# A product-based ranking network on one core: one set of row moves, fields by twos in the first three groups

## The reference, cut to what matters

```python
embed = tables[jnp.arange(26)[None, :], sparse_inputs]        # 2048 x 26 fields x 32, gathered
p   = jnp.einsum('bfe,bge->bfg', embed, embed)                 # inner products of all field pairs
l_z = jnp.einsum('bfe,feh->bh', embed, w_z)                    # 26*32 -> 256
l_p = jnp.einsum('bfg,fgh->bh', p, w_p)                        # 26*26 -> 256
l_1 = relu(concatenate([l_z + l_p + l_b, dense_inputs], -1))   # 256 + 13
h   = relu(l_1 @ W1 + b1)                                      # 128
return sigmoid(h @ Wf + bf)                                    # 2048 x 1
```

## Time and profile before

| | us |
|---|---|
| median of 3 runs | 598.29 |
| span of the profiled execution | 548.8 |
| median less span, what lies around it | 49.5 |
| busy POOL | 409.0 |
| busy DVE | 417.5 |
| busy ACT | 139.7 |
| busy PE (granted clock 0.683 in the mean) | 131.1 |

### The profile page before, as it was taken

One profiled execution on the slowest core, in us unless ns is written; L12 is line 12 of the kernel. 1 busy time (PEld: TensorE's weight loads), 2 busy tenths in 40 slices (PEclk: granted clock), 3 DMA queues, 4 the chain that ended last, 5 costly groups with the idle time before them and its releaser, 6 DMA issues.

```text
span 548.8 us, 1701 instructions
## 1 busy us (share of the span) xinstructions
PE 131.1 (24%) x204; PEld 48.0 (9%) x204; DVE 417.5 (76%) x250; ACT 139.7 (25%) x333; POOL 409.0 (75%) x430
## 2 busy tenths in 40 slices
PE   0000000415334100060465100051433600005067
PEld 0000000201111000020121000020110100002023
DVE  4204199998992369998996419999899547999995
ACT  0000004404551021704452010340455110250323
POOL 6777777777777777777777777777777777777792
PEclk9999999976567555585666655567665555558569
DMA  6222323122122222222112222222112222312220
GB/s 148 21 14 13 13 13 14 13 13 14 14 13 13 13 13 14 13 14 13 13 14 14 13 13 13 13 14 13 14 13 13 14 14 13 14 13 13 13 46 2
DMA packets 19640, 9.56 MB, mean 17 GB/s; under 512 B 9888, under 2 KB 19629, under 8 KB 19629
## 3 DMA queue, kind: packets, MB, share of 16 engines
q0 software_dynamic: 13312, 6.84, 22.4%
q1 hardware_dynamic: 6318, 2.63, 2.1%
HBM read 8.85 MB, written 0.01 MB: 16 GB/s over the span
## 4 chain that ended last, share of the span: by engine, by line
POOL 69%; issue 23%; DVE 6%; DMA 1%; PE 1%; ACT 0%; ACTq 0%; POOLq 0%; DVEq 0%
POOL rows L286 66%; DVE pairs L368 3%; DVE prod L348 2%; POOL prod L302 2%; POOL prod L313 1%; DMA rows<-in_L_rec_tables,which 1%; PE ps_h L643 0%; DMA raw<-in_r_sparse_inputs 0%; DVE pair_rows L404 0%; PE ps_h L680 0%; ACT scores L551 0%; PE ps_copy L692 0%; ACT hidden L537 0%; ACTq L120 0%; DVE pairs_T L395 0%
## 5 line engine op out<-in xcount | busy, mean ns | idle before, releaser
L286 POOL DMA_INDIRECT rows<-in_L_rec_tables,which x416 | 393.5, 946 | 128.4 <-issue 125.8
L348 DVE TENSOR_TENSOR prod<-ps_copy,rows 128x1664 f32<-128x1664 f32 (+12 forms) x103 | 194.2, 1910 | 16.8 <-ACT ps_copy L471 16.8
L368 DVE TENSOR_REDUCE pairs<-prod 128x76 f32<-128x2432 f32 (+13 forms) x73 | 195.3, 2680 | 0.0
L626 PE MATMUL ps_h<-field_rows,wz 128*128 128x512 f32 x96 | 59.4, 784 | 290.3 <-ACT field_rows L482 285.4
L379 DVE STREAM_TRANSPOSE rows_T<-rows 128x512 f32<-128x512 f32 (+1 forms) x28 | 18.6, 663 | 98.1 <-DMA rows<-in_L_rec_tables,which 90.7
L471 ACT COPY ps_copy<-rows 128x128 f32<-128x128 f32 (+2 forms) x63 | 21.2, 336 | 273.3 <-DMA rows<-in_L_rec_tables,which 273.0
L643 PE MATMUL ps_h<-pair_rows,w_pair 96*128 96x512 f32 (+2 forms) x64 | 50.2, 943 | 100.3 <-ACT pair_rows L505 84.4
L482 ACT COPY field_rows<-rows_T 32x512 f32<-32x512 f32 (+1 forms) x112 | 58.7, 524 | 34.9 <-DVE rows_T L379 33.4
L626 PEld LDWEIGHTS ps_h<-field_rows,wz 128*128 128x128 f32 x96 | 23.8, 258 | 328.0 <-issue 292.1
L505 ACT COPY pair_rows<-pairs_T 32x256 f32<-32x256 f32 (+1 forms) x96 | 33.5, 349 | 63.1 <-DVE pairs_T L391 61.9
L643 PEld LDWEIGHTS ps_h<-pair_rows,w_pair 96*128 96x128 f32 (+2 forms) x64 | 17.7, 296 | 130.4 <-ACT pair_rows L505 71.9
(11 more groups left out here) (37 smaller groups left out, 31.7 us busy)
## 6 DMA issues: line engine op xcount, KB each, us to landing
rows<-in_L_rec_tables,which POOLq DMA_INDIRECT x416, 3.4
wz<-in_L_rec_w_z SPq DMA_DIRECT2D x1, 768.0 KB, 5.8
field_rows<-rows_T SPq DMA_DIRECT2D x16, 32.0 KB, 1.9
w_pair<-in_w_low SPq DMA_DIRECT2D x1, 288.0 KB, 5.4
w_back<-in_w_high SPq DMA_DIRECT2D x1, 288.0 KB, 5.7
raw<-in_r_sparse_inputs SPq DMA_DIRECT2D x1, 156.0 KB, 2.2
w<-in_L_rec_W SPq DMA_DIRECT2D x1, 128.0 KB
dense_in<-in_r_dense_inputs SPq DMA_DIRECT2D x1, 104.0 KB, 3.2
```

Source lines behind the costliest of these rows:

```text
L286: nc.gpsimd.indirect_dma_start(rows[:, r % 2, f, k, :], None, table_rows, bass.IndirectOffsetOnAxis(ap=which[:, t, f:f + 1], axis=0),).the ...
L348: ins = nc.vector.tensor_tensor(products(r, s)[:, 0:tiles, at:at + g + 1, :], own.broadcast_to([P, tiles, g + 1, E]), rows[:, r % 2, 0:g + ...
L368: nc.vector.tensor_reduce(pairs[:, 0:tiles, first:end], products(r, s)[:, 0:tiles, :, :], AX.X, ALU.add)\
L626: ins = nc.tensor.matmul(ps_h0[:, h, :], wz[:, j, h * P:(h + 1) * P], field_rows[:, j, :, :, :].rearrange("p q t b -> p (q t b)"), start=( ...
```

## The change

- In groups 0 to 2 fields from 12 on are copied in units of two, and fields from 10 to 23 are multiplied and summed in stages of two; fields 24 and 25 stay single stages. The units per group go from 15 to 10, the stages from 18 to 12. The last group keeps its units and stages.
- In groups 0 to 2 the six row chunks are laid in one set (`MOVES`), by ACT after the group's last field copy, and the three pair blocks in one set (`PAIR_MOVES`) after them. The last group keeps its sets: chunks 0 to 3 by ACT, 4 and 5 by SP, pair blocks 0 and 1, then 2. PE's order follows.
- DVE waits for a free product buffer at every second stage (one stage further ahead), ACT for a free copy bank at every second unit (likewise).
- DVE's `turn_rows` no longer waits for the fields' landing itself, except for the last chunk of the last group, and stands after the multiply of the stage that holds the chunk's last field, in all four groups. `turn_pairs` and the pair sets are counted by group.
- The hidden layers and scores of the previous group are made behind fields 20, 22 and 24 (groups 1, 2) and 12, 13 and 14 (last group), instead of 0, 4 and 8.

```diff
-UNITS = [[(0, 4), (4, 8), (8, 12), (12, 14), (14, 16)] + [(f, f + 1) for f in range(16, 26)]] * (GROUPS - 1) + [FINE]
-STAGES = [[(0, 4), (4, 8), (8, 10), (10, 12), (12, 13), (13, 14)] + [(f, f + 1) for f in range(14, 26)]] * (GROUPS - 1) + [FINE]
+UNITS = [[(0, 4), (4, 8), (8, 12)] + [(f, f + 2) for f in range(12, 26, 2)]] * (GROUPS - 1) + [FINE]
+STAGES = [[(0, 4), (4, 8), (8, 10)] + [(f, f + 2) for f in range(10, 24, 2)] + [(24, 25), (25, 26)]] * (GROUPS - 1) + [FINE]
...
-    MOVES = [(0, 4), (4, MOVED), (MOVED, CH)]
-    NM = len(MOVES)
-    PAIR_MOVES = [(0, 2), (2, 3), (TAIL, TAIL + 1)]
+    LATE_MOVE = (4, MOVED)
+    MOVES = [(0, MOVED)] * (GROUPS - 1) + [(0, LATE_MOVE[0])]
+    NM = 2
+    PAIR_MOVES = [[(0, 3), (TAIL, TAIL + 1)]] * (GROUPS - 1) + [[(0, 2), (2, 3), (TAIL, TAIL + 1)]]
...
@@ multiply
-                if n >= PRODS:
-                    dve.wait_ge(summed, n - PRODS + 1)
+                if n >= PRODS - 1 and n % 2:
+                    dve.wait_ge(summed, n + 1 - PRODS + 1)
...
@@ turn_rows
-                for u in range(unit_of(r, PER * j), unit_of(r, PER * j + n - 1) + 1):
-                    first, end = UNITS[r][u]
-                    dve.wait_ge(landed[r][u], DMA * K * (end - first))
+                if r == ROUNDS - 1 and j == CH - 1:
+                    dve.wait_ge(landed[r][POOL_STAGE], DMA * K)
...
@@ DVE's loop
                     if s < len(STAGES[r]):
-                        for j in range(CH):
-                            if s == stage_of(r, UNITS[r][unit_of(r, PER * j + chunk_fields(j) - 1)][0]):
-                                turn_rows(r, j)
                         if r < ROUNDS - 1 or s != POOL_STAGE:
                             multiply(r, s)
+                        for j in range(CH):
+                            if s == stage_of(r, PER * j + chunk_fields(j) - 1):
+                                turn_rows(r, j)
                     if s:
                         add_up(r, s - 1)
...
@@ copy_fields
-                n = NU * r + u - COPIES
-                if n >= 0:
-                    before = r if u >= COPIES else r - 1
+                n = NU * r + u + 1 - COPIES
+                if n >= 0 and n % 2:
+                    before = r if u + 1 >= COPIES else r - 1
...
@@ ACT's loop, groups 0 to 2
                     if r and first == 0:
                         lay_last_pairs(r - 1)
+                    if r and first == 20:
                         make_hidden0(r - 1)
-                    if r and first == 4:
+                    if r and first == 22:
                         make_hidden1(r - 1)
-                    if r and first == 8:
+                    if r and first == 24:
                         make_scores(r - 1)
-                    if first in (14, 16, 17, 18):
-                        lay_rows(r, 0, (14, 16, 17, 18).index(first))
-                    if 20 <= first < 23:
-                        lay_pairs(r, 0, first - 20)
-                    if first == 23:
-                        lay_rows(r, SP_MOVE, 0)
-                    if first == 24:
-                        lay_rows(r, SP_MOVE, 1)
-                for q in range(2, QUADS):
-                    lay_rows(r, SP_MOVE, q)
+                for q in range(QUADS):
+                    lay_rows(r, q)
                 for u in range(PLACES):
-                    lay_pairs(r, 1, u)
+                    lay_pairs(r, 0, u)
                 lay_last_rows(r)
...
@@ ACT's loop, last group
                     lay_last_pairs(r - 1)
+                if first == 12:
                     make_hidden0(r - 1)
-                if first == 4:
+                if first == 13:
                     make_hidden1(r - 1)
-                if first == 8:
+                if first == 14:
                     make_scores(r - 1)
...
@@ PE's order
-                for j in range(*MOVES[0]):
+                for j in range(LATE_MOVE[0]):
                     sum_lz(r, j)
-                for c in range(*PAIR_MOVES[0]):
-                    sum_lp(r, c)
+                if r == ROUNDS - 1:
+                    for c in range(*PAIR_MOVES[r][0]):
+                        sum_lp(r, c)
                 sum_dense(r)
-                for j in range(*MOVES[1]):
+                for j in range(*LATE_MOVE):
                     sum_lz(r, j)
-                for c in range(*PAIR_MOVES[1]):
+                for c in range(0 if r < ROUNDS - 1 else PAIR_MOVES[r][0][1], TAIL):
                     sum_lp(r, c)

```

More of the change, by code:

```diff
@@ L99, in move_of, with pair_move_of @@
     def move_of(j):
-        return next(m for m, (first, end) in enumerate(MOVES) if first <= j < end)
-    def pair_move_of(c):
-        return next(m for m, (first, end) in enumerate(PAIR_MOVES) if first <= c < end)
+        return j // MOVED
+    def pair_move_of(r, c):
+        return next(m for m, (first, end) in enumerate(PAIR_MOVES[r]) if first <= c < end)
     def block_rows(c):
@@ L206, in pnn_kernel, with last_field @@
         MLP_LOADS = 6
-        PAIR_END = [BLOCK * PAIR_MOVES[0][1], BLOCK * PAIR_MOVES[1][1], NP]
-        FIELD_END = [next(g for g in range(NF) if pairs_before(g + 1) >= end) for end in PAIR_END]
+        def last_field(r, m):
+            first, end = PAIR_MOVES[r][m]
+            pairs_end = NP if first == TAIL else min(BLOCK * end, EARLY)
+            return next(g for g in range(NF) if pairs_before(g + 1) >= pairs_end)
         def ps_copy_bank(c):
@@ L242, in _ @@
             r = ROUNDS - 1
-            first, end = MOVES[SP_MOVE]
+            first, end = LATE_MOVE
             sp.wait_ge(rows_turned, CH * r + end)
@@ L383, in turn_pairs @@
             def turn_pairs(r, m):
-                first, end = PAIR_MOVES[m]
-                dve.wait_ge(summed, NS * r + stage_of(r, FIELD_END[m]) + 1)
-                if r == ROUNDS - 1 and m == NPM - 1:
+                first, end = PAIR_MOVES[r][m]
+                dve.wait_ge(summed, NS * r + stage_of(r, last_field(r, m)) + 1)
+                if r == ROUNDS - 1 and first == TAIL:
                     dve.wait_ge(pool_summed, 1)
                 if r:
-                    dve.wait_ge(pairs_laid, NPM * (r - 1) + m + 1)
+                    dve.wait_ge(pairs_laid, NPM * (r - 1) + pair_move_of(r - 1, first) + 1)
                 if first < TAIL:
@@ L442, in _ @@
                     if s < len(STAGES[r]):
-                        for j in range(CH):
-                            if s == stage_of(r, UNITS[r][unit_of(r, PER * j + chunk_fields(j) - 1)][0]):
-                                turn_rows(r, j)
                         if r < ROUNDS - 1 or s != POOL_STAGE:
                             multiply(r, s)
+                        for j in range(CH):
+                            if s == stage_of(r, PER * j + chunk_fields(j) - 1):
+                                turn_rows(r, j)
                     if s:
                         add_up(r, s - 1)
-                        for m in range(NPM):
-                            if stage_of(r, FIELD_END[m]) == s - 1:
+                        for m in range(len(PAIR_MOVES[r])):
+                            if stage_of(r, last_field(r, m)) == s - 1:
                                 turn_pairs(r, m)
@@ L472, in copy_fields, with lay_rows @@
                                rows[:, r % 2, first:end, :, :]).then_inc(copied, 1)
-            def lay_rows(r, m, q):
-                first, end = MOVES[m]
+            def lay_rows(r, q):
+                first, end = MOVES[r]
                 if q == 0:
@@ L510, in lay_last_pairs @@
             def lay_last_pairs(r):
-                act.wait_ge(pairs_turned, NPM * (r + 1))
+                act.wait_ge(pairs_turned, NPM * r + len(PAIR_MOVES[r]))
                 for u in range(LAST):
@@ L584, in _ @@
                     lay_last_pairs(r - 1)
+                if first == 12:
                     make_hidden0(r - 1)
-                if first == 4:
+                if first == 13:
                     make_hidden1(r - 1)
-                if first == 8:
+                if first == 14:
                     make_scores(r - 1)
                 if 15 <= first < 19:
-                    lay_rows(r, 0, first - 15)
+                    lay_rows(r, first - 15)
                 if 22 <= first < 24:
@@ L620, in sum_lz @@
                     pe.wait_ge(hidden0_made, HALVES * r)
-                if r == ROUNDS - 1 and move_of(j) == SP_MOVE:
+                if r == ROUNDS - 1 and j >= LATE_MOVE[0]:
                     pe.wait_ge(rows_moved, DMA * QUADS * PER)
@@ L634, in sum_lp @@
                     pe.wait_ge(w_pair_made, 1)
-                pe.wait_ge(pairs_laid, NPM * r + pair_move_of(c) + 1)
+                pe.wait_ge(pairs_laid, NPM * r + pair_move_of(r, c) + 1)
                 if c == TAIL:
-                    pe.wait_ge(rows_laid, NM * (r + 1) - (1 if r == ROUNDS - 1 else 0))
+                    pe.wait_ge(rows_laid, NM * (r + 1))
                     if r == ROUNDS - 1:
```

3 lines of the change are left out of this document (1 added, 2 removed).

## The result

The changed kernel takes 619.45 us (median of 4, 618.97 to 619.84) beside 598.37 us for the kernel before: ratio 1.0349, 95% interval 1.0336 to 1.0361, slower. The forecast was 601.3, the range 599.2 to 604.6; the sign was right, the size was not.

A forecast was written before the change was run, and what follows sets the result against it. POOL's gathers were taken to bound groups 0 to 2, the last group's tail the end. All else priced 0, the later turns added 3.06 us: span 548.8 + 3.1 = 551.9, plus 49.5 outside, 601.3 us, range 599.2 to 604.6.

The forecast's parts named there:

- 49.5 us lie around the span; unchanged: Outside the profiled span of 548.8 us: the rest of the 598.29 us median, 49.5 us, stays as it was.
- (b): Rival: the 49.5 us outside the span shrink with fewer instructions and semaphores, time 594.2 to 597.8 us; chance 0.15.
- So one every 518.9 / 415 = 1.25 us on the mean: POOL's 416 gathers start at this steady pace from 3.6 to 522.5 us, hiding what groups 0 to 2 compute.
- The MLP of group 2 ... Price 0, bounds 0 and +0.5: Group 2's hidden layers and scores, moved to last-group fields 12, 13 and 14 on ACT, cost 0, at most 0.5 us.
- rows and pairs in one set: Groups 0 to 2: ACT issues 84 fewer row and block copies, 16 us in all, hidden behind gathers and priced at 0.
- The turn at field 23, +3.06: Last group, chunk 5: DVE's turn after the multiply delays SP's 16 DMAs and PE, so the tail starts 3.06 us later.
- The turn at field 15, +0.33: Last group, chunk 3: the later turn delays ACT's copy of field 16, adding 0.33 us to DVE's chain, bounds 0 and 0.7.
- The clock: PE's late matmuls: duration kept as it was; bounds -1.7 us if fast throughout, +3.4 and +1.8 if slow throughout.
- rival (a): PE's clock stays low through the late burst: 601.3 + 1 to 5 us, centre 604; chance 0.14.
- The waits: DVE's product-buffer and ACT's copy-bank waits at every second stage or unit: price 0; for DVE bounds -0.3 and 0.
- rival d: ACT's bunched copies at a group's end hold back group 3 beyond DVE's idle: up to +2.3 us, 603.6; chance 0.04.

The follow-up runs named there:

- e10: Changed kernel with the last group's hidden layers and scores behind fields 18, 20 and 22 and DVE's turn before the multiply: 598.73 us, ratio 0.9997.
- e18: Changed kernel with groups 0 to 2 leaving out the matmuls of pair blocks 0 to 2 but for one column per block: 607.69 us, ratio 1.0156.
- e16: The changed kernel itself, run again where the kernel before takes 550.69 us: 553.69 us, ratio 1.0057.
- e4: Changed kernel with the buffer waits at every stage and unit again: 620.55 us, ratio 1.0358.
- e13: Kernel before with only the last group's hidden layers and scores moved behind fields 12, 13 and 14: 550.54 us, ratio 0.9997.
- e17: Repeat of e13, the kernel before with the last group's hidden layers and scores behind fields 12, 13 and 14: 550.67 us.
- e1: The kernel before, unchanged, profiled a second time: 599.02 us, ratio 0.9999.
- e6: Changed kernel with the last group's hidden layers and scores behind fields 18, 20, 22 and DVE's turn before the multiply: 550.71 us, ratio 1.0000.
- e11: Changed kernel in which POOL waits before gathering the last group's field 13 until group 2's hidden layer has been made: 610.81 us.

## Why the prediction was wrong, step by step

**"49.5 us lie around the span; unchanged"** is the step that failed first. Only 2.2 us lie around a span (618.97 against 616.8). The other 47 us were inside the timed executions and were missing in the one profiled: 37.8 us of them are later gathers, and 10.0 us a longer end behind the last gather (36.3 against 26.3). By itself this step moved no number, since 598.29 + 3.06 is 601.3 either way; but it kept condition L out of sight, in which the missing cost arises. A gap of 8% was taken for a constant, and one rival was even built on it (b). (That rival's count was off too: 1701 instructions became 1463, so 238 fewer and not about 120, because waits count as instructions as well.) The gap should have been read as a sign that the profile was of another kind of execution than the times.

**"So one every 518.9 / 415 = 1.25 us on the mean"** was true of that execution. In L it is 1.25 us up to about 220 us, then 1.4. This costs both kernels alike (37 to 38 us), so it does not explain the ratio; it comes in the same condition as what does.

**"The MLP of group 2 ... Price 0, bounds 0 and +0.5"** is the step that missed the size. It counted ACT's own instructions and took for granted that PE's sums of group 2 would release the layer long before field 12. The sums are indeed complete by then (464.7 against 490). But PE's completion is not ACT's release: in L the two are 58 us apart, once "rows and pairs in one set", priced at 0 as well, had drawn PE's five spaced bursts of a group together into 84 records. The measured cost in place of the 0 is ACT's stall of 32.6 us, of which 18.0 us reach the end. Each half of the cause was weakened by itself: a later place (e10) gives back the 18.0 us, and a shorter burst (e18, 12 records fewer) 11.8 us.

**The turn at field 23, +3.06**: right in mechanism and in size. The turn was forecast at 524.6 and measured at 524.27 in e16; SP's first DMA at 525.3 and 525.00; PE's row sums at 537.0 and 536.68; the total is +3.0 in K by the medians. The two profiled executions differ by 2.3: PE's row sums start 3.2 us later and not 3.57, and its last 16 records take 0.4 us less than worked out. In L the term is 2.7.

**The turn at field 15, +0.33**: the late copy of field 16 is in e16 too (multiply of field 16 at 482.13, of 17 at 486.66), but of field 17's start nothing remained, and DVE's tail transposes start at 539.75, as before at 539.77; the 0.33 was used up by slack.

**The clock**: PE's 8 records took 5.31 us in e16 against 5.49 before; rival (a) did not occur there, and in L the 8 took 5.75 us.

**The waits**: priced at 0, with a gain of 0.3 us as the bound; e4 shows a gain of 0 to 1 us and does not settle it.

**The late bunches of ACT** (rival d): in e16 group 3's first field copy stands at 421.60, where 421.8 was worked out, and costs nothing.

So the forecast of a slower kernel came true in L for the larger part by another cost than the one that was priced: 3 of the 20 to 21 us were foreseen. In K the sum came out in full, 553.7 us where 550.7 + 3.06 is 553.8.

**Left open.** What the records wait for in L, and why some chips are in L and others in K. The trace shows the spacing only. Each run of the experiments has a span beside its time, so its instructions were recorded, and no run shows whether the delay exists without the recording. Whether the moved place alone would cost anything in the kernel before in L was not seen, since e13 and e17 ran in K; with the lag of 0.2 us that e1 shows it should not, but this is argued. No version beat the kernel before in either condition: e6 and e10 tie with it (1.0000 and 0.9997).

## What to carry to other kernels

When the span of the profile and the times differ by far more than the 2.2 us seen here, the profile is likely of another kind of execution: profile again before pricing anything. A signal need not be as early as the end of the instruction that sends it (58 us in L, under 0.1 us in K). Joining work into one burst may delay every signal behind it, so put a consumer in an in-order engine where it can afford the lag, or keep the producer's bursts short. A reorder in one engine's program should be followed to the DMA issues that wait on it: here moving one 0.7 us transpose behind a 3.3 us multiply cost 3.0 us of 550.

## What the runs showed that was not expected

- Two conditions of the same program: 550.7 to 550.8 and 598 to 599 us for the kernel before, with all runs taken on one chip together within 0.3%.
- In the longer one, gathers go from one per 1.25 us to one per about 1.4 us at about 220 us, in every kernel tried, and back to 1.25 us after a pause of 28 us (e11).
- In it, ACT's copies at a group's end start 0.84 and 0.52 us apart for 22 or 23 instructions and then 1.40 us apart, whatever their own length (0.3 to 0.6 us). In K the same copies go on at 0.52 and 0.31 us.
- In it, PE's semaphore rises stand 1.40 us apart for each record: 11.2 us where K has 1.7. A PE burst of 84 records delays PE's signal by 58.3 us, one of 72 by 40.1 us; with the gathers paused the rest of the delay passes about 1.4 times faster (36.4 us in 26.7).
